# Counting edges in 80 strips of 8 destinations instead of 40 windows of 16

## The reference, cut to what matters

```python
def layer0(x, W, a, src, dst):
    h = x @ W
    al, ar = h @ a[0, :d], h @ a[0, d:]
    e = exp(-leaky_relu(al[src] + ar[dst], 0.1))
    rowsum = segment_sum(e, src)
    h_prime = segment_sum(e[:, None] * h[dst], src) / (rowsum[:, None] + 1e-5)
    return elu(h_prime)

def layer1(x, src, dst, type, weight, root, bias, w_gate, b_gate):
    u = x @ root + bias
    for r in range(8):
        mask = type == r
        sums = segment_sum(x[src] * mask[:, None], dst)
        u = u + (sums / maximum(segment_sum(mask, dst), 1)[:, None]) @ weight[r]
    z = concatenate([u, x], 1) @ w_gate + b_gate
    return tanh(u) * z + x * (1 - z)

x = layernorm(x + layer0(x, ...))
x = layernorm(x + layer1(x, ...))
```

## Time and profile before

| what | us |
|---|---|
| three runs, lowest, median, highest | 1004.27, 1005.56, 1006.47 |
| the profiled execution, its own time | 1005.25 |
| its span, first to last instruction | 1003.4 |
| PE busy | 990.5 (99%) |
| PE weight load busy | 836.8 (83%) |
| DVE busy | 391.1 (39%) |
| ACT busy | 278.0 (28%) |
| POOL busy | 254.1 (25%) |

### The profile page before, as it was taken

How to read it: one execution, slowest core, us unless ns; L and a number is a source line. 1 busy time by engine, 2 the same in 40 slices (tenths; PEclk the granted TensorE clock), 3 DMA queues, 4 the chain that set the end, 5 groups by cost and what they waited for, 6 DMA issues and landing times.

```text
span 1003.4 us, 14843 instructions
## 1 busy us (share of the span) xinstructions
PE 990.5 (99%) x5272; PEld 836.8 (83%) x5272; DVE 391.1 (39%) x746; ACT 278.0 (28%) x477; POOL 254.1 (25%) x196
## 2 busy tenths in 40 slices
PE   9999999999999999999999999999999999999997
PEld 7777678878888888888988888988988888888886
DVE  6887973541430520430341232232232233112277
ACT  4332453761221221221221222212212212212332
POOL 0000002036423223223132142231231231326730
PEclk9999999999999999999999999999999999999999
DMA  7114557055311411321331131141051041212402
GB/s 262 53 57 124 150 146 249 1 202 164 117 45 43 139 54 43 117 73 42 107 84 42 68 120 35 31 159 41 12 170 42 21 159 42 73 43 74 137 1 102
DMA packets 69005, 91.42 MB, mean 91 GB/s; under 512 B 9396, under 2 KB 35475, under 8 KB 68838
## 3 DMA queue, kind: packets, MB, share of 16 engines
q1 hardware_dynamic: 68966, 90.90, 29.0%
HBM read 75.19 MB, written 15.69 MB: 91 GB/s over the span
## 4 chain that ended last, share of the span: by engine, by line
PE 95%; DVE 2%; ACT 1%; issue 0%; POOL 0%; DVEq 0%; ACTq 0%
PE ps L1164 21%; PE ps L1166 21%; PE ps L1165 21%; PE ps L1385 9%; PE ps L1384 9%; PE ps L1244 6%; PE ps L1211 2%; PE ps L1439 1%; PE ps L1440 1%; PE ps L1438 1%; PE ps L1219 1%; PE ps L1188 1%; PE ps L1221 1%; PE ps L1220 1%; PE ps L1373 0%
## 5 line engine op out<-in xcount | busy, mean ns | idle before, releaser
L457 POOL TENSOR_TENSOR w_lo<-w_raw,w_hi 128x512 fp32r<-128x512 f32 x168 | 217.3, 1298 | 707.3 <-ACT w_hi L532 548.6
L532 ACT CAST w_hi<-w_raw 128x512 fp32r<-128x512 f32 x184 | 114.8, 624 | 459.9 <-PE ps L1166 388.9
L1164 PE MATMUL ps<-w_hi,M_hi 128*128 128x512 f32 (+1 forms) x560 | 221.1, 395 | 0.1
L1166 PE MATMUL ps<-w_lo,M_hi 128*128 128x512 f32 (+1 forms) x560 | 219.0, 391 | 0.0
L1165 PE MATMUL ps<-w_hi,M_lo 128*128 128x512 f32 (+1 forms) x560 | 218.8, 391 | 0.0
L1038 DVE SCALAR_TENSOR_TENSOR u<-ps,scale,u 128x512 f32<-128x512 f32 (+1 forms) x90 | 66.4, 745 | 315.5 <-PE ps L1166 315.5
L1384 PE MATMUL ps<-C_hi,x_hi 128*128 128x320 f32 (+3 forms) x640 | 184.4, 306 | 0.0
L1385 PE MATMUL ps<-C_hi,x_lo 128*128 128x320 f32 (+3 forms) x640 | 184.3, 306 | 0.0
L1164 PE MATMUL ps<-w_hi,M 128*128 128x512 f32 (+1 forms) x360 | 140.3, 390 | 0.0
L1166 PE MATMUL ps<-w_lo,M 128*128 128x512 f32 (+1 forms) x360 | 140.2, 390 | 0.0
L1165 PE MATMUL ps<-w_hi,M 128*128 128x512 f32 (+1 forms) x360 | 140.2, 389 | 0.0
(11 more groups left out here) (169 smaller groups left out, 776.8 us busy)
## 6 DMA issues: line engine op xcount, KB each, us to landing
w_raw<-weights SPq DMA_DIRECT2D x184, 256.0 KB, 2.8
C_dram<-Cst SPq DMA_DIRECT2D x25, 512.0 KB, 6.0
C_hi<-C_dram SPq DMA_DIRECT2D x8, 1600.0 KB, 6.8
z<-b_gate SPq DMA_DIRECT2D x5, 512.0 KB, 9.7
u<-bias SPq DMA_DIRECT2D x5, 512.0 KB, 7.4
xT_raw<-xT SPq DMA_DIRECT2D x8, 312.5 KB, 6.7
u<-x SPq DMA_DIRECT2D x4, 512.0 KB, 5.0
last_raw<-weights SPq DMA_DIRECT2D x8, 256.0 KB, 5.9
```

The lines of the kernel that those rows point to most:

```text
L457: pool.tensor_tensor(w_lo[k % RING][:, :], w_raw[k % RING][:, :], w_hi[k % RING][:, :].bitcast(f32), ALU.subtract).then_inc(w_lo_done, 1)
L532: nc.scalar.copy(w_hi[k % RING][:, :], w_raw[k % RING][:, :]).then_inc(w_hi_done, 1)
L1164: mm(o, lhs_hi[:, k, c], w_hi[k % RING][:, :], start=opens, stop=False)
L1166: last = mm(o, lhs_hi[:, k, c], w_lo[k % RING][:, :], start=False, stop=closes_)
```

## The change

`WIN` is halved to 8 destinations, so a window becomes two strips of 320 codes each. A pass treats 3 tiles; three sets of three slots are used in turn, each with semaphores of its own. A strip has one PSUM bank (5 or 6, in turn) and ACT copies it by itself. The relations are summed with the identity as the weights and `Cst` as the moving operand, 384 or 256 columns at a time (`sum_counts`), copied by ACT to `all_r` (`copy_summed`) and then turned, one matmul per source block (`turn_sums`). `AHEAD` is 5 chunks, and the other 15 items stand in seven windows of two strips. The last three weight splits, all `low_h` and seven dots move to the first window on DVE. At the start the warming matmuls are 8 of 512 columns instead of 26 of 128, the first two chunks go through PE in rounds (all high x high, then low x high, then high x low), and SP loads weights and x in turn.

```diff
     TILES = dst_cols.shape[1]
-    BODY = 5
+    BODY = 3
+    SETS = 3
     ALL_TILES = -(-TILES // BODY) * BODY
     STARTS = ALL_TILES - BODY + 1
     LOOP_END = STARTS * (ALL_TILES // BODY)
     SUB = 2
     UNITS = dst_units.shape[0]
-    WIN = P // R
-    WINDOWS = NP // WIN
-    PER = P // WIN
+    WIN = P // R // 2
+    STRIPS = NP // WIN
+    STRIPS_PER = P // WIN
+    WINDOWS = STRIPS // 2
+    PER = STRIPS_PER // 2
     CODES = NT * R
+    HOT = CODES * WIN
     SPLIT = NP // 2
...
-        AHEAD = 2
-        SPREAD = 15
-        WARM = 26
+        AHEAD = 5
+        SPREAD = 7
+        DOTS_AHEAD = 7
+        WARM = 8
 
         def items(w):
             lo, hi = [AHEAD * NT + (KT - AHEAD) * NT * v // SPREAD for v in (w, w + 1)] if w < SPREAD else (ALL, ALL)
             return [divmod(i, NT) for i in range(lo, hi)]
...
-                    load_chunk(0, k, first=True)
+                load_chunk(0, k, first=k < RING)
                 sp.dma_start(xT_raw[:, k, :], xT[k * P:(k + 1) * P, :]).then_inc(xT_here[k], 16)
-                if k == 2:
+                if k == RING - 1:
                     sp.dma_start(units_i[:, :], dst_units).then_inc(edges_here, 16)
                     sp.dma_start(ints[:, 0, :], dst_cols).then_inc(edges_here, 16)
                     sp.dma_start(ints[:, 1, :], src_cols).then_inc(edges_here, 16)
                     sp.dma_start(ints[:, 2, :], type_cols).then_inc(edges_here, 16)
             sp.dma_start(a_bc[:, :], a[0, :].partition_broadcast(P)).then_inc(a_here, 16)
-            load_ahead(0)
+            for k in range(RING):
+                load_chunk(1, k)
             load_ahead(1)
...
+
+            def copy_strip(n):
+                j, v = divmod(n, STRIPS_PER)
+                act.wait_ge(strip_counted, n + 1)
                 if v == 0 and j >= 2:
                     act.wait_ge(flushed[j - 2], 16 * NT)
                     act.wait_ge(turned, 2 * (j - 1))
-                nc.scalar.copy(Cst[j % 2][:, :, :, v * WIN:(v + 1) * WIN].rearrange("p m r d -> p (m r) d")
-                               .rearrange("p (b q) d -> p b q d", b=2),
-                               ps[:, window_bank(w) * H2:(window_bank(w) + 2) * H2]
-                               .rearrange("p (b n) -> p b n", b=2)[:, :, 0:SPLIT]
-                               .rearrange("p b (q d) -> p b q d", d=WIN)).then_inc(window_copied, 1)
+                nc.scalar.copy(Cst[j % 2][:, :, :, v * WIN:(v + 1) * WIN].rearrange("p m r d -> p (m r) d"),
+                               bank(5 + n % 2, c=HOT).rearrange("p (q d) -> p q d", d=WIN)).then_inc(strip_copied, 1)
+
+            def copy_summed(j, part):
+                m0, m1 = turn_blocks(part)
+                act.wait_ge(summed, 2 * j + part + 1)
+                act.wait_ge(turned, 2 * j + part)
+                nc.scalar.copy(all_r[:, 0:(m1 - m0) * P], bank(turn_bank(j, part), c=(m1 - m0) * P)).then_inc(summed_read, 1)
 
             def copy_turned(j, part):
...
-            def hots(w):
-                n = dve.snap(turn, min_val=1, max_val=WINDOWS * ALL_TILES)
+            def hots(n):
+                b = n % SETS
+                use = dve.snap(turn[b], min_val=1, max_val=STRIPS * ALL_TILES)
                 tile = dve.snap(tile_at, min_val=0, max_val=ALL_TILES - BODY)
                 for s in range(BODY):
-                    dve.wait_ge(counted[s], n)
-                    v.tensor_scalar(hot[:, s * NP:(s + 1) * NP], table[:, :], float(WIN * w),
-                                    key[:, ds(tile + s, 1)], ALU.add, ALU.is_equal).then_inc(built[s], 1)
-                dve.reg_add(turn, turn, 1)
+                    dve.wait_ge(counted[b][s], use)
+                    v.tensor_scalar(hot[:, (b * BODY + s) * HOT:(b * BODY + s + 1) * HOT], table[:, 0:HOT], float(WIN * n),
+                                    key[:, ds(tile + s, 1)], ALU.add, ALU.is_equal).then_inc(built[b][s], 1)
+                dve.reg_add(turn[b], turn[b], 1)
                 dve.reg_add(tile_at, tile_at, BODY)
 
             for w in range(WINDOWS):
-                first_pass = window_range(DVE_ENGINE, w)
-                dve.reg_mod(tile_at, first_pass, STARTS)
-                with dve.Fori(first_pass, LOOP_END, STARTS + BODY):
-                    hots(w)
-                if w < RING - 1 - AHEAD:
-                    split_low(1, AHEAD + w)
-                for k in range(RING - 1, KT):
-                    if w == SPLIT_AT[k] + 1:
-                        split_low(1, k)
-                if w < NT:
-                    low_h(w)
-                if NT <= w < 3 * NT:
-                    t, lr = divmod(w - NT, 2)
-                    if w == NT:
-                        dve.wait_ge(a_here, 16)
-                    else:
-                        dve.wait_ge(dot_done, w - NT)
-                    dot(0, lr, t, h_raw[0:rows(t), t, :], h_part(1, 1, NT - 1))
+                for n in range(2 * w, 2 * w + 2):
+                    first_pass = strip_range(DVE_ENGINE, n)
+                    dve.reg_mod(tile_at, first_pass, STARTS)
+                    with dve.Fori(first_pass, LOOP_END, STARTS + BODY):
+                        hots(n)
+                if w == 0:
+                    split_low(1, AHEAD)
+                    for t in range(NT):
+                        low_h(t)
+                    split_low(1, AHEAD + 1)
+                    dve.wait_ge(a_here, 16)
+                    for n in range(DOTS_AHEAD):
+                        dot_raw(n)
+                    split_low(1, AHEAD + 2)
+                elif w <= 2 * NT - DOTS_AHEAD:
+                    dot_raw(DOTS_AHEAD + w - 1)
...
+            def chunk_rounds(k):
+                cols = [slice(t * P, t * P + rows(t)) for t in range(NT)]
+                outs = [bank(xw_bank(t), rows(t)) for t in range(NT)]
+                pe.wait_ge(xT_hi_done, k + 1)
+                pe.wait_ge(w_hi_done, k + 1)
+                for t in range(NT):
+                    if k == 0:
+                        pe.wait_ge(u_drained, t + 1)
+                    mm(outs[t], M_hi[0][:, k, cols[t]], w_hi[k][:, :], start=k == 0, stop=False)
+                pe.wait_ge(xT_lo_done, k + 1)
+                for t in range(NT):
+                    mm(outs[t], M_lo[0][:, k, cols[t]], w_hi[k][:, :], start=False, stop=False)
+                pe.wait_ge(w_lo_done, k + 1)
+                for t in range(NT):
+                    last = mm(outs[t], M_hi[0][:, k, cols[t]], w_lo[k][:, :], start=False, stop=False)
+                last.then_inc(w_used, 1)
+
             pe.wait_ge(ones_set, 1)
             for _ in range(WARM):
-                mm(bank(6, c=P), ones_r[:, :], ones_r[:, :], start=True, stop=True)
-            chunk_items(0, 1, 2)
+                mm(bank(6).rearrange("p (a b) -> p a b", b=P), ones_r[:, :],
+                   ones_r[:, :].unsqueeze(1).broadcast_to([P, H2 // P, P]), start=True, stop=True)
+            chunk_rounds(0)
+            chunk_rounds(1)
+            chunk_items(2)
+            chunk_items(3)
             pe.wait_ge(units_diag_done, 1)
             for c in range(2):
...
-            def turn_counts(j, part, blocks=None):
+            def sum_counts(j, part):
                 m0, m1 = turn_blocks(part)
-                pe.wait_ge(window_copied, PER * (j + 1) + 1)
+                pe.wait_ge(strip_copied, STRIPS_PER * (j + 1) + 1)
                 if turn_bank(j, part) == 4:
                     pe.wait_ge(turned_read, 2 * j + part)
-                for m in blocks or range(m0, m1):
-                    for r in range(R):
-                        last = mm(bank(turn_bank(j, part), c0=(m - m0) * P, c=P), Cst[j % 2][:, m, r, :], ident_r[:, :],
-                                  start=r == 0, stop=r == R - 1)
-                if m == m1 - 1:
-                    last.then_inc(turned, 1)
+                o = bank(turn_bank(j, part), c=(m1 - m0) * P).rearrange("p (m n) -> p m n", n=P)
+                for r in range(R):
+                    last = mm(o, ident_r[:, :], Cst[j % 2][:, m0:m1, r, :], start=r == 0, stop=r == R - 1)
+                last.then_inc(summed, 1)
+
+            def turn_sums(j, part):
+                m0, m1 = turn_blocks(part)
+                pe.wait_ge(summed_read, 2 * j + part + 1)
+                for m in range(m1 - m0):
+                    last = mm(bank(turn_bank(j, part), c0=m * P, c=P), all_r[:, m * P:(m + 1) * P], ident_r[:, :], start=True, stop=True)
+                last.then_inc(turned, 1)
 
...
-            def counts(w):
-                n = pe.snap(turn, min_val=1, max_val=WINDOWS * ALL_TILES)
+            def counts(n):
+                b = n % SETS
+                use = pe.snap(turn[b], min_val=1, max_val=STRIPS * ALL_TILES)
                 edge = pe.snap(edge_at, min_val=0, max_val=(ALL_TILES - BODY) * P)
                 for s in range(BODY):
-                    pe.wait_ge(built[s], n)
-                    for c in range(2):
```

(97 more changed lines are left out.)

73 lines of the change are left out of this document (38 added, 35 removed).

## The result

The changed kernel takes 1030.83 us (median of four runs, 1027.67 to 1031.32) against 1005.25: ratio 1.0248, 95% interval 1.0228 to 1.0269. It is 25.6 us slower. I had forecast 12 slower.

The account below looks back on a forecast made before the run. PE's sequencer was taken to bound the strips: 50.9 + 108.8 + 2.4 + 12 + 2 - 1.6 = 174.5 us at the loop's end, 13.7 later; less 1.7 makes +12.0, so 1017 us, range 1001 to 1031.

Parts of the forecast that it names:

- moved chunks turn the change sour: Ahead of the loop: 15 items, 45 matmuls, moved there fill no sequencer time; the loop starts 10.0 us later.
- the price of a strip: Counting loop: PE's sequencer takes 1.36 us a strip, bounds 1.30 and 1.45; 108.8 us for 80.
- start of the loop: Before the loop: 44.45, plus 10.0 for chunks ahead, less 3.6 for shorter warming and earlier full pace, gives 50.9 us.
- four second passes: Strips needing two passes: the second skips the register load, about 0.6 us each, 2.4 us.
- slow loads: Strips during four flushes of `Cst`: 20 register loads 0.65 us longer, taken as 12 us, bounds nothing and 18.
- waits, less the head start: In the loop: about 16 new waits before sums and turns, 2 us; sequencer running two strips ahead gives 1.6 back.
- loop's end to the end, against before: After the loop: identity sums with fewer, wider matmuls save 1.7 us.
- bare window of before: Old loop, two windows with nothing between: 1.7 us from load to load on PE's sequencer, the basis for a strip.
- Rival (c): Counting loop: TensorE's clock drops to its lower level in idle gaps, 10 us more, 1027 us; chance 0.15.
- signs of being wrong: Loop: later windows at 2.3 us or less, PE waiting more for `hot` or `Cst` than issue, or the clock column falling.
- Rival (a): Counting loop: the sequencer is not the limit, DVE is; 973 us at best, 985 with half; chance 0.15.
- rival (b): Flush stretches: register loads stay at 0.30 us, 12 us less, 1005.5 us, within noise of no change; chance 0.15.

Follow-up runs that it names:

- three fillers: The changed kernel with three more matmuls of 320 columns by zeros behind the counts of every strip: 1029.18 us, ratio 1.0239.

## Why the prediction was half right

**The mechanism held, the size did not.** The loop is bound by PE's sequencer; items, sums and turns are covered by it; moved chunks turn the change sour. Each is shown above. What failed is the sizes: the price of a strip and of a second pass, and the clock, which stood only among the rivals. The steps, in the profiled executions (forecast 1015.4 of span, measured 1029.5):

| step | forecast, us | measured, us |
|---|---|---|
| start of the loop | 50.9 | 51.4 |
| 80 strips | 108.8 at 1.36 | 114.4 at 1.43 |
| four second passes | 2.4 | 5.2 |
| slow loads | 12 | 10.2 |
| waits, less the head start | 0.4 | 5.3 |
| loop's end to the end, against before | -1.7 | +0.4 |

The measured rows of the loop are 80 x 1.43, the second passes, the sum over slow loads, and what is left of 135.1. Three of the second passes make their steps 1.43, 1.26 and 1.35 us longer, slow loads taken off; the fourth falls into the sequencer's head start and is put at their mean. They are one profiled execution's.

**The first step that failed is the price of a strip.** The bare window of before gave 1.7 - 2 x 0.125 = 1.45. I went below it for three missing matmuls, because a step without one behind it had taken 0.1. The measured 1.43 shows that the matmuls cost the sequencer almost nothing: 5.6 us. And 1.43 is the price of an undisturbed strip; 21 of the 56 quiet steps take 1.46 to 1.70 and the mean is 1.47, which puts some 3 us more into the waits of the table.

**The second is the second pass.** I priced PE's sequencer, 0.6. But both passes of a strip use the same set of slots. DVE may write the one-hots of the second only when PE has counted those of the first, and PE's sequencer then waits for them. The timeline of DVE at the last of them:

```profile
180.59 0.84 DVE L927 TENSOR_SCALAR hot<-table,key 128x320 bf16<-128x320 f16 x3 [2.99 <-PE ps L1280]
182.03 0.73 DVE L927 TENSOR_SCALAR hot<-table,key 128x320 bf16<-128x320 f16 x3 [0.59 <-issue]
```

DVE had idled for 2.99 us until PE's first count, begun at 180.00, was done. It compares from 180.59, and PE's next count starts at 181.04, 1.04 us behind the first; with the clock held by three fillers that way is 0.90 (180.86 to 181.76). A second pass costs this way back and forth, 2.8 us more than forecast over the four. Whether a set of its own for the second pass would save it was not tried. A comparison in a row takes 0.24 us (0.73 for three), where I took 0.2 from between 0.155 and 0.31; elsewhere that was covered: the 0.6 us in the list of waits is all that PE's array idles for one-hots in the loop.

**The third is that I made the clock a rival and not a part.** Rival (c) came true beside the forecast. I gave it 10 us; it cost about 3, as the sequencer covers the slower array except where something waits for the array itself. Such a place is the window at 131.5: six attention products at 0.43 us and then sums that wait for copies; from that load to the next is 3.2 us, against 2.1 at the same place with the clock held by three fillers. PE's loads there, of the changed kernel and of that with three:

```profile
L323 PEldq TENSOR_LOAD <-lohi_row x2: 298/630/961, 131.5 to 134.7; - x2
```

```profile
L323 PEldq TENSOR_LOAD <-lohi_row x2: 324/628/933, 132.8 to 134.9; - x2
```

Behind the loop it costs 2.4 and eats the 1.7 that the identity sums save. So one of my signs of being wrong came true, the falling clock column; and PE idles for 25.5 us of the loop and not 45, in part because at the lower clock the same matmuls keep it busy longer. The page of the Trainium skill that spoke for it, "TensorE: Matmul & The Clock Gate", section "A second HAM failure mode: psum-queue depth-cycling", was right that the clock would swing where matmuls come in groups with gaps between: the trace has 0.56 to 1.00 in stretches of 10 us. That the cycling of PSUM banks makes the gaps no run shows; here they are the sequencer's.

**What held.** Slow loads: 15 over 0.6 us where I said 18 to 20, 10.2 us with the one of 0.55 for 12. That taking them away gave 9.3 and not 12 follows from the same sum. The start, within 0.5 us: I took off 3.6, as 2.0 for the shorter warming and 1.6 for an earlier full pace. No run measures the 1.6 apart; together they gave 3.0 (51.4 against 44.45 + 10.0), and the first products run at the full pace at once. The floor of about 600 ns that the Trainium skill's "DMA: Bandwidth & Descriptors", section "Latency and other measured facts", gives does not hold here: PE's fastest of 80 loads takes 295 ns. Rival (a) fell with the 1.43 us between loads, rival (b) with the slow ones.

**One reading that misled.** I took PE's 8.04 busy of 10 us in 107.5 to 117.5 as a sign of the sequencer. The same row has DVE at 9.96, and at 10.00 in the stretch before: comparisons and drains fill DVE, and it is the bound there. The 1.7 us of the bare window, on which my price rests, is the sequencer's: there each one-hot is ready when its step comes, the closest by 0.04 us, and the steps follow each other without a wait.

**What stays open.** The 5.3 us of other waits are a remainder, of one execution. The loads give it places: the step at 131.5 is 1.8 us over 1.43 (1.1 of it by the clock, the difference just shown), the one at 117.3 is 0.9 (the wait for ACT's copy named above), some 3 us are spread over the quiet steps, and the head start takes 1.6 off. Why some quiet steps are 0.1 us longer than others was not looked into, nor the clock's share of what is left.

## What to carry to other kernels

Before halving a tile inside a loop with runtime bounds, measure the sequencer's time of one pass, from one register load to the next in a stretch with nothing between; it is paid per pass, and halving the tile left 1.43 of 1.7 us here. If twice that is more than the array's work in a whole window, the array's saving cannot show. Price it straight from that stretch, and take off only the steps that go; where the array is left idle, add the clock as a cost on whatever still waits for the array, not as an alternative.

## What the runs showed of the hardware

- A register load from SBUF takes 0.30 us, and 0.55 to 1.08, mostly over 0.9, while a flush of the counts to memory runs; without the flush none in the loop is slow. On PE it holds up the sequencer for all of that time, even when its register is read a strip later.
- On PE's sequencer the step is the same 1.43 us whether three counting matmuls behind it take 0.58 us (full clock) or 0.98 (1.2 GHz).
- The granted clock was 1.00 up to 80 us and fell in the stretch 80 to 90, in a flush, where strips are longest. One matmul of 320 columns more in each strip raised the loop's mean from 0.78 to 0.87, three to 0.99.
